# A graph network's aggregation with table parts as stationary operands: A moves for four tiles at once, the own term joins its diagonal

## What is computed

```python
deg  = segment_sum(ones, rows) + 1.0
dinv = rsqrt(deg)[:, None]
h = x @ W_in + b_in
for l in range(4):
    msg = segment_sum((h * dinv)[cols], rows) * dinv
    global_ctx = mean(h, axis=0) @ Wg[l] + bg[l]
    z = relu((h + msg) @ Wl[l] + bl[l] + global_ctx)
    h = (z - mean(z)) * rsqrt(var(z) + EPS) * gamma[l] + beta[l]
```

## Time and profile before

| | |
|---|---|
| runs | 3126.79 us median of 3 (3126.16 to 3127.82) |
| the profiled execution | 3126.55 us, its span 3124.9 us |
| TensorE busy | 2998.0 us, 96% of the span |
| DVE busy | 1943.2 us, 62% |
| ACT busy | 949.0 us, 30% |
| the aggregation's matmuls (L1647) | 9604 of 128 x 512, 2142.0 us busy |
| layers, first matmul to last | 533.2 to 2797.2 us |

### The profile page before, as it was taken

One profiled execution on the slowest core, in us unless ns is written; L12 is line 12 of the kernel. 1 busy time (PEld: TensorE's weight loads), 2 busy tenths in 40 slices (PEclk: granted clock), 3 DMA queues, 4 the chain that ended last, 5 costly groups with the idle time before them and its releaser, 6 DMA issues.

```text
span 3124.9 us, 55195 instructions
## 1 busy us (share of the span) xinstructions
PE 2998.0 (96%) x18038; PEld 1697.4 (54%) x18038; DVE 1943.2 (62%) x5237; ACT 949.0 (30%) x2112; POOL 78.0 (2%) x169
## 2 busy tenths in 40 slices
PE   6999996999999999999999999999999999988998
PEld 5777774444444444444444444444444444445776
DVE  8999997555555555555555555555566666666676
ACT  5898887111111111111111111111111111116765
POOL 0000000000000000000000000000000000000111
PEclk9999997999999999999999999999999999998999
DMA  4333325222222222122221222212222222211000
GB/s 132 89 87 88 88 82 139 77 85 85 92 79 82 85 79 71 63 71 72 72 72 62 72 72 72 71 63 71 74 84 78 78 84 84 84 38 43 23 25 26
DMA packets 138137, 233.87 MB, mean 75 GB/s; under 512 B 13717, under 2 KB 105988, under 8 KB 138018
## 3 DMA queue, kind: packets, MB, share of 16 engines
q1 hardware_dynamic: 131058, 217.55, 21.4%
q10 hardware_dynamic: 4608, 8.39, 0.8%
q0 software_dynamic: 2352, 6.40, 0.7%
HBM read 186.58 MB, written 45.74 MB: 74 GB/s over the span
## 4 chain that ended last, share of the span: by engine, by line
PE 83%; ACT 10%; DVE 4%; issue 3%; DVEq 0%; DMA 0%; ACTq 0%; SPq 0%; POOL 0%; POOLq 0%
PE bank L1647 66%; ACT tab L1270 8%; PE bank L1605 4%; PE bank L1749 4%; PE bank L1732 4%; PE bank L1595 1%; PE bank L1495 1%; DVE later L812 1%; PE bank L1515 1%; DVE region L779 1%; PE bank L1541 1%; ACT later L1294 0%; PE bank L1535 0%; PE bank L1745 0%; ACT xnb L1288 0%
## 5 line engine op out<-in xcount | busy, mean ns | idle before, releaser
L1647 PE MATMUL bank<-tab,region 128*128 128x512 f16 x9604 | 2142.0, 379 | 17.3 <-DMA region<-adjacency 17.3
L1647 PEld LDWEIGHTS bank<-tab,region 128*128 128x128 fp8e4 x9604 | 940.5, 98 | 1067.6 <-DVE tab L896 19.6
L1270 ACT ACTIVATE tab<-later 128x539 fp8e4<-128x539 uint8 x588 | 336.1, 674 | 1.9 <-DVE later L812 1.9
L779 DVE TENSOR_SCALAR region<-iota_w,src_col,src_w 128x540 bf16<-128x540 int16 x858 | 310.4, 413 | 0.4 <-issue 0.2
L1373 ACT ACTIVATE sd<-mv,eps_c 128x1 f32<-128x1 f32 x196 | 57.7, 295 | 811.2 <-DVE mv L1011 811.2
L1004 DVE SCALAR_TENSOR_TENSOR region<-bank,c_back,later 128x256 f32<-128x256 f32 x196 | 94.8, 484 | 331.5 <-PE bank L1605 331.5
L995 DVE TENSOR_TENSOR region<-bank,region 128x256 f16<-128x256 f32 x196 | 83.2, 425 | 287.4 <-ACT region L1369 287.4
L1369 ACT ACTIVATE region<-bank 128x256 f16<-128x256 f32 x196 | 75.3, 384 | 567.5 <-PE bank L1595 567.5
L1367 ACT ACTIVATE region<-bank 128x256 f32<-128x256 f32 x196 | 75.3, 384 | 305.4 <-PE bank L1647 305.4
L1605 PE MATMUL bank<-later,region 128*128 128x256 f16 x1176 | 160.7, 273 | 0.9 <-DVE region L995 0.9
L1337 ACT ACTIVATE tab<-region,c_write 128x256 f32 (+1 forms) x147 | 74.7, 508 | 268.6 <-DVE region L1020 268.6
(11 more groups left out here) (235 smaller groups left out, 2421.1 us busy)
## 6 DMA issues: line engine op xcount, KB each, us to landing
region<-adjacency SPq DMA_DIRECT2D x196, 784.0 KB, 4.3
adjacency<-tab SPq DMA_DIRECT2D x12, 3136.0 KB, 13.9
region<-in_x POOLq DMA_DIRECT2D x48, 128.0 KB, 2.3
out<-region SPq DMA_DIRECT2D x48, 128.0 KB, 1.7
tab<-in_x SPq DMA_DIRECT2D x5, 1024.0 KB, 11.9
dstf<-in_L_ffn_W ACTq DMA_DIRECT2D x16, 256.0 KB, 2.6
srcf<-in_L_ffn_W ACTq DMA_DIRECT2D x16, 256.0 KB, 2.9
tab<-in_L_ffn_W SPq DMA_DIRECT2D x4, 512.0 KB, 4.9
```

The source lines that it names most:

```text
L779: v.tensor_scalar(hot_s[:, j, :], iota_w[:, 0:WP], src_col[:, ds(first_block[0] + j, 1)], src_w[:, ds(first_block[0] + j, 1)], ALU.is_equa ...
L1270: ins = a.activation(stage[h][:, :, slot, f * LANES:f * LANES + n], counts[:, :, 0:n], ACT.Copy, saturate=False)
L1647: ins = mm(acc[a][:, :], A_s[:, a, m, :], tab[:, here + m, :], start=m == 0, stop=m == T - 1)
```

## The change

The operands change places. The stationary operand is now a 128 x 128 part of the table (four for each source: high and low, two halves of the features), and the moving one is the fp8 row of A for **four** destination tiles, 512 columns. The sums come out with features on the partitions, which is what the product's stationary operand needs. So `turn_u`, the copy of the low half, `hs`, `acc_s`, `Q` and U go away. ACT and DVE now split a group's sums straight from two PSUM banks (`high_sums`, `split`), two instructions each for a group.

- The 49 tiles are 14 groups: eleven of four tiles, one of three (44 to 46), two of one tile (47, 48).
- The own term is an integer: (h + msg) is proportional to the degree times the own row plus A's sum. So 49 diagonal blocks `degree * identity + A[t, t]` are made once in f16 (`diagonal`, DVE), from 49 small loads (`own_blocks`, 128 x 128 bytes each, SP). Where a group meets its own tile as a source, the 512 columns are cut into the tiles ahead of it, those behind it, and the diagonal block.
- A's buffer holds **one group**, in seven chunks of seven sources (448 KB each). A group goes over the chunks in the order of their numbers, save that the chunks that hold its own tiles come last, and its own tiles are the last sources of all. A chunk's load for the next group waits for `a_used` of that chunk. SP asks for the chunks as 0, 1, ... 6.
- Products of a group's tiles run in the following group, at sources 4, 14, 24, 34 (other places for the last groups). In layer 0's first group, the weights' bound stands before the 31st source, `mean` before the 32nd, `context` before the 37th. The order of its chunks is 1 to 6, then 0, and two of A's chunks are now asked for ahead of the layers' weights.
- In the first stage, the write of A's last four columns is cut in two, TensorE does the last product of h0 ahead of the degrees and the last mean behind the flag.

```diff
 # SP
-                    def load(n, t, i, a):
-                        sp.wait_ge(agg_done, n + 1)
-                        sp.dma_start(A32_s[:, a, :],
-                                     A[ds(t, 1), :, :, :].rearrange("o p m s -> (o p) (m s)")).then_inc(a_in[a], 16)
+            def own_blocks():
+                for t in range(T):
+                    sp.dma_start(own_a[:, t * P // 4:(t + 1) * P // 4].bitcast(I32),
+                                 A[t:t + 1, :, t:t + 1, :].rearrange("o p m s -> (o p) (m s)")).then_inc(own_in, 16)
+                def load(gi, g, t0, w, c):
+                    sp.dma_start(A32_s[:, c, 0:w, :],
+                                 A[ds(t0, w), :, c * SEVEN:(c + 1) * SEVEN, :].rearrange("d p m s -> p d (m s)")
+                                 ).then_inc(a_in[c], 16)
+                def load_group(gi, g, t0, w):
+                    for c in range(T // SEVEN):
+                        sp.wait_ge(a_used[c], gi)
+                        load(gi, g, t0, w, c)
...
+                for c in FIRST_ORDER:
+                    load(0, 0, 0, GROUP, c)
+                    if c == FIRST_ORDER[1]:
+                        layer_weights()
+                own_blocks()
 # DVE
+            def diagonal(t):
+                v.scalar_tensor_tensor(out=diag_of(t), in0=ident[:], scalar=degp[:, t:t + 1], in1=own_a8[:, t, :], op0=ALU.mult,
+                                       op1=ALU.add).then_inc(diag_ready, 1)
+            dve.wait_ge(own_in, 16 * T)
+            for t in range(T // 2):
+                diagonal(t)
...
+            for t in range(T // 2, T):
+                diagonal(t)
+            dve.wait_ge(diag_ready, T)
             dve.sem_inc(wx_ready, 1)
...
+                def split(gi, pair, w, col):
+                    for k in range(KC):
+                        dve.wait_ge(s_high, gi * KC + (k + 1))
+                        v.scalar_tensor_tensor(out=sT[:, 1, k, col * P:(col + w) * P], in0=sums[pair][k][:, 0:w * P],
+                                               scalar=s_scale[:], in1=sT[:, 0, k, col * P:(col + w) * P], op0=ALU.mult,
+                                               op1=ALU.subtract).then_inc(s_low, 1)
 # ACT
+                def high_sums(gi, free, pair, w, col):
+                    act.wait_ge(agg_done, gi + 1)
...
+                    for k in range(KC):
+                        a.activation(sT[:, 0, k, col * P:(col + w) * P], sums[pair][k][:, 0:w * P], ACT.Copy,
+                                     scale=s_scale[:]).then_inc(s_high, 1)
 # TensorE
-                        ins = mm(acc[a][:, :], A_s[:, a, m, :], tab[:, here + m, :], start=m == 0, stop=m == T - 1)
+                    late = [c for c in range(T // SEVEN) if any(m // SEVEN == c for m in mine)]
+                    order = [c for c in range(T // SEVEN) if c not in late] + late
+                    order = [m for c in order for m in range(c * SEVEN, (c + 1) * SEVEN) if m not in mine] + list(mine)
...
+                        for b in range(2):
+                            for k in range(KC):
+                                f = (b * KC + k) * P
+                                parts = [(A_s[:, c, 0:w, m % SEVEN, :], 0, w)]
+                                if own is not None:
+                                    parts = [(A_s[:, c, d0:d1, m % SEVEN, :], d0, d1)
+                                             for d0, d1 in ((0, own), (own + 1, w)) if d0 < d1]
+                                    parts.append((diag_of(m), own, own + 1))
+                                for moving, d0, d1 in parts:
+                                    ins = mm(to[k][:, d0 * P:d1 * P], tab[:, here + m, f:f + P], moving,
```

More of the change, by code:

```diff
@@ L79 @@
 TURN_AT, PRODUCT_AT = 0, 8
-BEFORE_T, BEFORE_MM = 14, 24
+GROUP = 4
+STARTS = tuple(range(0, 48, GROUP)) + (47, 48)
+WIDTHS = (GROUP,) * 11 + (3, 1, 1)
+GROUPS = len(STARTS)
+PAIRED = (0, 1) * 6 + (2, 1)
+COLUMN = (0,) * 12 + (3, 0)
+LOOPED = 5
+FIRST_ORDER = (1, 2, 3, 4, 5, 6, 0)
+PIECES = 32
+FULLEST = 2040.0
+BOUND_M, MEAN_M, CONTEXT_M = 30, 31, 36
+PRODUCTS_AT = {"first": {4: 48, 20: "mean", 24: "context"}, "four": {4: 0, 14: 1, 24: 2, 34: 3},
+               "three": {5: 0, 17: 1, 29: 2, 41: 3}, 12: {8: 44, 34: 45}, 13: {10: 46, 36: 47}}
 def hold(eng, sem, value):
@@ L209, in build @@
         at[0] = 0
[L210 to L218, removed]
@@ L837, in _ @@
             dve.wait_ge(deg_done, MG + 1 + T + 1)
-            own.done(v.reduce_sum(bad[:], bank[6][:, 0:T], AX))
+            own.done(v.tensor_scalar(degp[:], bank[6][:, 0:T], FULLEST, None, ALU.min))
+            own.wait()
+            own.done(v.reduce_sum(bad[:], degp[:], AX))
             own.wait()
@@ new lines, in split, with norm @@
+                def split(gi, pair, w, col):
[4 more added lines that the diff above has]
+                                               op1=ALU.subtract).then_inc(s_low, 1)
+                def norm(n, t, g, d, between=None):
+                    late = last and not (isinstance(t, int) and t == 0)
@@ new lines, in scanned @@
+                def scanned(*to):
+                    group(*to, scan=first)
+                one_group(scanned, l, 0)
+                one_group(scanned, l, 1)
+                looped_groups(act, scanned, l, 1, PIECES // (2 * GROUP))
+                for g in range(PIECES // GROUP, 2 * LOOPED + 1):
+                    one_group(group, l, g)
+                n0, t0 = l * T + STARTS[11], STARTS[11]
+                high_sums(l * GROUPS + 11, n0, PAIRED[11], WIDTHS[11], COLUMN[11])
+                norm(n0, t0)
@@ L1652, in rest, with product_of, between @@
-                def rest(l):
-                    with pe.Fori(0, LOOP) as i:
-                        for a in range(RING):
-                            aggregate(l, l * T + i * RING + a + 1, a, i, l)
+                def product_of(l, g, t):
+                    pe.wait_ge(s_low, 4 + (l * GROUPS + g + 1) * KC)
+                    product_u(l * T + t, l, COLUMN[g] + t - STARTS[g])
+                def between(l, g, q):
+                    if g == 0 and l == 0:
+                        if q == BOUND_M:
+                            weight_bound()
+                        elif q == MEAN_M:
+                            mean(0)
+                        elif q == CONTEXT_M:
+                            context(0)
+                    elif g == 0:
+                        what = PRODUCTS_AT["first"].get(q)
+                        if what == "mean":
+                            mean(l)
+                        elif what == "context":
+                            context(l)
+                        elif what is not None:
+                            product_of(l - 1, 13, what)
+                    elif g <= 11:
+                        what = PRODUCTS_AT["four" if g < 11 else "three"].get(q)
+                        if what is not None:
+                            product_of(l, g - 1, STARTS[g - 1] + what)
+                    else:
+                        what = PRODUCTS_AT[g].get(q)
+                        if what is not None:
+                            product_of(l, 11 if what < 47 else 12, what)
@@ L1657, in fast @@
                 for l in range(LAYERS):
[L1658 to L1661 removed]
+                    for g in range(GROUPS):
+                        group(l, g)
+                product_of(LAYERS - 1, 13, T - 1)
             def general():
@@ L1683, in general @@
+                    looped_groups(pe, group, l, 0, LOOPED)
+                    for g in range(2 * LOOPED, GROUPS):
+                        one_group(group, l, g)
                 for l in range(LAYERS):
```

458 lines of the change are left out of this document (279 added, 179 removed).

## The result

The changed kernel takes **3144.99 us**, median of 4 runs (3143.3 to 3150.2), against 3127.10 us (3126.16 to 3127.82, 4 runs) before: 1.0059 times as long, 95% interval 1.0045 to 1.0072. The forecast was 3144.

The account below looks back on a forecast made before the run. TensorE, busy 96% of the span with no gap in a tile's row, was taken as the bound. Terms -41.7 + 6 + 39 + 14 + 1 - 3 + 1.5 = +17 on 3126.55 gave 3144 us; range 3096 to 3174.

Parts of the forecast that it names:

- transposes, more and narrower matmuls, products: TensorE in the layers: transposes gone -41.7 us, more and narrower matmuls +6, a product waiting for its split +1.
- A's loads: TensorE waits for chunks at each layer's second, third and fourth group: 9.8 us a layer, +39 us in four.
- the clock behind them: Slow 1.2 GHz clock after waits for A: 2.0 us at second groups, 1.6 at third, +14 us in all.
- ahead of layer 0: Start of layer 0: TensorE starts earlier but waits 12.5 us for the context; first group ends near 586, -3 us.
- the end: From last sum to mean: transposes and copies gone, but two tiles' norms queue on DVE; about 13 us, +1.5.
- the third rival: One-tile groups: loads of weights bind, a pair at 98 ns, 66 us more, 3210 us; chance 0.03.
- The third term: Wait for A at a layer's fourth group, whose late chunk's load stands behind another's: 0.6 us.
- the last of the rivals: Fp8 as moving operand slower than f16, or TensorE's unrolled program comes too slowly: over 3172 us; chance 0.04.
- The first rival: Layers: no waits for A, chunks being asked for early enough; only -36 us left, 3090 us; chance 0.16.
- The second: Rival: A's seven chunk loads share bandwidth and land together, 12.8 us at second groups, 3225 us; chance 0.07.
- group 2 pays 1.6: Third group of each layer: its 2.6 us wait drops the clock, costing 1.6 us each time.
- 49 loads at 0.36 each 17.6: Ahead of layer 0: SP asks for 49 diagonal blocks in 17.6 us, at 0.36 each; landed by about 551.

Follow-up runs that it names:

- the early mean: Changed kernel with ACT copying layer 0's mean into a free tile, before it waits for weights and diagonals: 3120.78 us, 0.9978 of the kernel before.
- the single load: Changed kernel with its 49 small loads of diagonal blocks put into one DMA: 3132.60 us, 1.0018 of the kernel before.
- the two orders: Changed kernel with SP asking for chunks as they come back, and TensorE's third group taking the late chunk later: 3091.00 us, 0.9884 of the kernel before.
- with the transposes: Changed kernel with two unused f32 transposes of 128 x 128 added before each product: 3187.79 us, 1.0196 of the kernel before.
- both orders and the early mean: Changed kernel with SP's and TensorE's chunk orders changed and layer 0's mean copied ahead of the waits: 3077.97 us, 0.9848 of the kernel before.
- the seven edits: All follow-up runs, each an edit of the changed kernel (load orders, mean copy, added transposes, one DMA, combinations): from 3068.34 to 3187.79 us.
- the first experiment: Changed kernel with only SP's order changed, asking for chunks as the group before gives them back: 3105.96 us, 0.9930 of the kernel before.

## Why the prediction was right, step by step

The forecast held in time, sign and mechanism: the gain of the transposes is real, and the queue of SP takes it back. That it came within 1 us is luck: the errors of the terms in the table below add up to 15 us without their signs, and to 1 with them.

| term | predicted | measured |
|---|---|---|
| transposes, more and narrower matmuls, products | -34.7 | -39.0 |
| A's loads | +39 | +37.8 |
| the clock behind them | +14 | +12.0 |
| ahead of layer 0 | -3 | +3.1 |
| the end | +1.5 | +1.0 |
| feed-forward stage | 0 | +1.0 |
| sum | +17 | +15.9 (the spans differ by 16.9) |

- **The gain in the layers.** From the first product of layer 0's second group (603.94) to that of layer 1's (1169.92) are 565.98 us; less two waits and the cold clock (6.73 + 2.83 + 2.69) a layer takes 553.73. Before, 191 tiles with three layer boundaries took 2194.26 (596.70 to 2790.96), so (2194.26 - 191 x 11.45) / 3 = 2.4 for a boundary and 49 x 11.45 + 2.4 = 563.5 for a layer: 9.75 less, 39.0 in four. The transposes alone are 41.7 to 42.8. A full group of 44.98 is 0.03 over 45.80 less four transposes, so cutting it around its own tiles costs 1.3 in all and not 3. The groups of one tile cost 196 x 0.0559 + 0.66 = 11.61 against 11.24 without transposes, 3 us for eight, as predicted. The wait of 1 us at the group of tile 47 is at most 0.3: the products' idle time is 2.0 in the whole run, and 1.7 of it is the last product's. That leaves 1.6 of the 39.0 at the layers' boundaries, half of it the 0.8 for which the contexts of layers 1 to 3 waited before; the other half isn't accounted for. Pieces and pairs were only read from the trace, with no run of their own.
- **Loads of weights don't bind.** Pairs of 128 columns follow at 0.0559 us, so the third rival (3210) is out. The Trainium skill's rule that was set against it (TensorE: Matmul & The Clock Gate, "LDWEIGHTS (loading the stationary operand)") gives 107 ns for such a load and doesn't hold here. The same page of the Trainium skill says of a full 128-column load that isn't f32 that it goes about twice as fast ("Weight-path perf modes — Fast Weight Load (FWL) and DoubleRow"), which is near the pace measured. The fp8 moving operand with f16 weights runs at f16's pace, 0.216, which takes out the last of the rivals.
- **A's loads.** Per layer the sum had 6.6, 2.6 and 0.6 at the second, third and fourth group; measured were 6.4 to 6.8, 2.8 to 2.9, and none. The third term was near the edge: in other versions with SP's old order the fourth group did wait 0.7 to 0.9 us in some layers (once with the early mean, three times with the single load). The reason in the sum (the first chunk asked for is the last given back) was tested by the two orders: with it gone, the waits are gone. The first rival (3090, no waits) is what the kernel becomes then: 3091.0. The second (seven loads share the engines, 12.8 us) is out.
- **The clock.** The step "group 2 pays 1.6" each time was wrong: behind the short wait the clock fell in one layer of four, and cost 2.9 there. Behind the long wait it took 2.3 on average, for 2.0. The row that the step was read from the earlier trace rows goes both ways itself: at the same place in the feed-forward stage, behind the same 2.40 us of idle time, 18 matmuls took 4.5 to 4.8 us in the changed kernel and four of its edits, and 3.1 with the clock up in two others (with the transposes, and with both orders and the early mean).
- **Ahead of layer 0.** The failed step is "49 loads at 0.36 each 17.6". They took 25.3, 0.515 each, the own blocks came at 556.8 and not at 551, and the context could start at 576.3 and not at 570.9. The chain (loads, diagonals, flag, ACT's copy) was right: cut at the copy it gave 24 us, shortened at the loads 12. The wait is 9.7 us longer than the 12.5 of the sum, but 4.3 of that cost nothing: TensorE came to the context sooner (554.1 for 558.4), having started at 520.5 for 524, and could only wait there. The other 5.4 moved the group's end, to 591.6 for the 586 of the sum. Of the +3.1, 2.3 are that end with three products still owed (591.6 + 2.0 - 591.3), and 0.8 the gain of group 0 that the first line of the table already counts.
- **The end** was right: +1.0 for +1.5, by DVE's queue of two tiles. The feed-forward stage, from the mean (2824.61, before 2808.70) to the span's end, is 1.0 longer: 317.2 against 316.2. In the seven edits, which leave it alone, it takes 316.3 to 317.6, so nothing here tells the 1.0 from chance.

## What to carry to other kernels

When one buffer in pieces takes the place of several whole ones, the order in which an in-order queue asks for the pieces must be the order in which they come free, and the reader's order must leave the last piece for last: here that was 50 us, more than the gain of the whole idea. A short thing that others wait for (a copy of a mean) should not share a flag with a long one, and many small DMAs on one queue are paid for in the asking. Gains found one at a time overlap; after each, look again at which wait ends last.

## What the runs showed of the hardware

- **The clock behind idle times of 2.4 to 3.2 us fell in some cases and held in others.** At the third group's wait it fell in 1 of 4 layers of the changed kernel, 2 of 4 in the first experiment, 1 of 4 with the early mean, all 4 with the transposes, none of 4 with the single load. Length doesn't sort them: one of 2.65 us lost it (first experiment, 639.89), one of 3.15 us kept it (1758.47, with the early mean, 16 matmuls in 3.61). What does sort them no run shows. Behind all 16 waits of 6.2 to 7.6 us at the second group it was down. The price was 1.3 to 2.9 us.
- **Small DMAs cost SP 0.515 us each**, 49 in 25.26 us, about what a load of 448 KB cost it (two in a row, 0.94). One DMA with all 6272 pieces of 128 bytes took SP 1.13 us to ask for, and landed 9.5 us later; a small one landed 1.8 us later.
- **fp8 as the moving operand beside f16 weights** goes at the pace of f16: 0.216 us for 512 columns.
